# First batch's projection, residual and statistics, and the turned expansion weights, placed in the attention's last steps

## What is computed

```python
x = x + _L0_attn_ref(_layernorm(x), W_attn, W_proj, lambdas)   # differential attention, 16 heads
x = x + _L0_ffn_ref(_layernorm(x), W_syn, b_syn, W_out, b_out, gamma, beta)
...
# in the attention
out = (1.0 - LAMBDA_INIT) * out.reshape(B, T, E)
return out @ W_proj
# in the feed-forward part
z = x_flat @ ternary_quant(W_syn).T + b_syn        # 256 -> 1024
thresh = topv[:, -1:]                              # 102nd largest of each row
hidden = jnp.where(z >= thresh, jax.nn.relu(z), 0.0)
out = hidden @ ternary_quant(W_out).T + b_out      # 1024 -> 256
return layernorm(x + out, gamma, beta)
```

## Time and profile before

| What | Value |
|---|---|
| median of 3 runs | 1247.23 us (1247.14 to 1247.43) |
| the profiled execution, its own time | 1245.16 us |
| its span, first to last instruction | 1243.3 us |
| mean granted TensorE clock | 0.942 of full speed |
| PE busy | 1090.3 us (88%) |
| DVE busy | 908.9 us (73%) |
| ACT busy | 629.1 us (51%) |
| POOL busy | 217.8 us (18%) |

### The profile page before, as it was taken

How to read it: one execution, slowest core, us unless ns; L and a number is a source line. 1 busy time by engine, 2 the same in 40 slices (tenths; PEclk the granted TensorE clock), 3 DMA queues, 4 the chain that set the end, 5 groups by cost and what they waited for, 6 DMA issues and landing times. The chain is left out here.

```text
span 1243.3 us, 18349 instructions
## 1 busy us (share of the span) xinstructions
PE 1090.3 (88%) x7006; PEld 754.3 (61%) x7006; DVE 908.9 (73%) x1699; ACT 629.1 (51%) x1098; POOL 217.8 (18%) x172
## 2 busy tenths in 40 slices
PE   2969999999999878777868569999997899999998
PEld 2823333333333347656757457888886789889986
DVE  7778999999999424689888576555553788897833
ACT  2526878788787852876631133333333433433324
POOL 6004400000000001000033204000000744654400
PEclk9969999999999989998988769999999899999979
DMA  2871133033120010000000111101100100000010
GB/s 93 201 240 31 23 53 52 3 52 52 24 31 3 1 39 1 1 1 1 1 1 1 34 56 34 30 22 35 35 1 15 45 1 1 2 1 1 2 64 6
DMA packets 24850, 40.02 MB, mean 32 GB/s; under 512 B 3116, under 2 KB 12344, under 8 KB 24760
## 3 DMA queue, kind: packets, MB, share of 16 engines
q1 hardware_dynamic: 24760, 38.82, 13.0%
HBM read 28.06 MB, written 10.49 MB: 31 GB/s over the span
## 5 line engine op out<-in xcount | busy, mean ns | idle before, releaser
L667 DVE TENSOR_REDUCE att_mx<-att_ps_m 128x2 f32<-128x1024 f32 x256 | 311.0, 1225 | 23.8 <-PE att_ps_m L561 20.2
L650 ACT ACTIVATE att_prob<-att_ps_s 128x512 f32<-128x512 f32 x512 | 278.2, 596 | 79.3 <-PE att_ps_s L589 66.6
L605 PE MATMUL att_ps_o<-att_prob,v_rows 128*32 128x256 f32 (+1 forms) x1920 | 159.4, 405 | 0.0
L1767 POOL TENSOR_TENSOR qry_prod<-qry_qr,lin_ksum 128x512 f32<-128x512 f32 x64 | 93.8, 1466 | 306.5 <-ACT qry_qr L1888 306.5
L589 PE MATMUL att_ps_s<-qst,kst 50*128 50x512 f32 x512 | 128.1, 496 | 13.6 <-ACT att_prob L650 12.6
L589 PEld LDWEIGHTS att_ps_s<-qst,kst 50*128 50x128 f32 x512 | 48.2, 183 | 126.9 <-ACT att_prob L650 117.2
L561 PE MATMUL att_ps_m<-kst,qst 48*128 48x512 f32 x512 | 110.0, 424 | 9.0 <-DVE att_mx L667 7.2
L1888 ACT ACTIVATE qry_qr<-qry_ps_q 128x512 f32<-128x512 f32 x64 | 38.3, 598 | 131.0 <-PE qry_ps_q L152 114.6
L1468 DVE SCALAR_TENSOR_TENSOR key_k_lo<-key_ps_k,key_k_hi 128x512 fp32r<-128x512 f32 x64 | 44.2, 690 | 67.8 <-ACT key_k_hi L1548 67.3
L605 PEld LDWEIGHTS att_ps_o<-att_prob,v_rows 128*32 128x32 f32 x1920 | 38.2, 108 | 84.5 <-ACT att_prob L650 71.4
L1068 ACT ACTIVATE mlp_junk<-mlp_z,mlp_nlev 128x1024 bf16<-128x1024 f32 x64 | 72.7, 1139 | 23.0 <-DVE mlp_nlev L904 21.5
(11 more groups left out here) (364 smaller groups left out, 2448.2 us busy)
## 6 DMA issues: line engine op xcount, KB each, us to landing
qst<-qk_parts SPq DMA_DIRECT2D x48, 128.0 KB, 4.3
kst<-qk_parts SPq DMA_DIRECT2D x48, 128.0 KB, 6.8
qk_parts<-att_out SPq DMA_DIRECT2D x16, 256.0 KB, 5.5
qk_parts<-qk_lo SPq DMA_DIRECT2D x16, 256.0 KB, 5.7
residual<-L_attn_x SPq DMA_DIRECT2D x4, 512.0 KB, 6.0
lin_wq_raw<-L_attn_Wk SPq DMA_DIRECT2D x4, 512.0 KB, 3.6
lin_wq_raw<-L_attn_Wv SPq DMA_DIRECT2D x4, 512.0 KB, 3.6
lin_wq_raw<-L_attn_Wq SPq DMA_DIRECT2D x4, 512.0 KB, 5.8
```

The lines of the kernel that those rows point to most:

```text
L605: ins = nc.tensor.matmul(ps_o[32 * h:32 * h + 32, cols], vall[:, NS * b + s, h0 + h, :], prob[:, u % PR, h, cols], start=s == 0, stop=s == ...
L650: nc.scalar.activation(prob[:, u % PR, 2 * j + r, :], ps_s[:, (n + r) % BANKS, :], ACT.Exp).then_inc(exp_ok, 1)
L667: nc.vector.reduce_max(mx[:, v % 2, :, m], ps_m[:, n % 2], AX.X).then_inc(m_rd, 1)
L1767: nc.gpsimd.tensor_tensor(prod[:, u % 2, :], qr[:, u % 2, :], ksum[:, b, cols(n)], ALU.mult).then_inc(pr_ok, 1)
```

## The change

A new class `FeedFront` holds, from the attention on, W_proj (`ff.wp`), the turned chunk (`ff.at`), the turned W_syn (`ff.ws_t`) and the norm's work for chunks 0 and 1 (`ff.norms`). Six side units are added to the attention's table, all for buffers `ps_m`: "syn" 0 and 1 in steps 117 and 118, "turn" 0 in step 119, "proj" 0 in 120, "turn" 1 in 121, "proj" 1 in 122. VectorE evacuates each; behind a "proj" it also makes the statistics. W_proj is loaded at the attention's start. The feed-forward stage then has neither the prologue for chunk 0 nor, in step 0, that for chunk 1; it only makes the two roots. It starts with a clearing of the attention's semaphores on SyncE.

```diff
+        u = NS * (HALVES - 1) - LEAD + 1
+        for k in range(d.KT):
+            side[u + k].append(("syn", k, 0))
+        for c in range(ff.CHUNKS):
+            side[u + d.KT + 2 * c].append(("turn", c, 0))
+            side[u + d.KT + 2 * c + 1].append(("proj", c, 0))
...
+                sp.dma_start(ff.wp[:], io["L0_attn_W_proj"].rearrange("(k p) n -> p k n", p=P)).then_inc(wp_in, 16)
                 load_group(1)
...
+                    elif kind == "syn":
+                        pe.wait_ge(tern_ok, 1)
+                        for a in range(d.N // P):
+                            ins = nc.tensor.matmul(ps_m[:, n % 2].rearrange("p r c -> p (r c)")[:, a * P:(a + 1) * P],
+                                                   tern[:, 0, a * d.E + v * P:a * d.E + (v + 1) * P],
+                                                   keep["ident_b"][:], start=True, stop=True)
+                    elif kind == "turn":
+                        for k in range(d.KT):
+                            for j in range(d.TPC):
+                                ins = nc.tensor.transpose(ps_m[:, n % 2, k, j * P:(j + 1) * P],
+                                                          AO[:, d.TPC * v + j, k * P:(k + 1) * P], ident[:])
+                    elif kind == "proj":
+                        pe.wait_ge(wp_in, 16)
+                        pe.wait_ge(m_rd, place("turn", v))
+                        for j in range(d.TPC):
+                            dst = ps_m[:, n % 2].rearrange("p r c -> p (r c)")[:, j * d.E:(j + 1) * d.E]
+                            for k in range(d.KT):
+                                ins = nc.tensor.matmul(dst, ff.at[:, k, j * P:(j + 1) * P], ff.wp[:, k, :],
+                                                       start=k == 0, stop=k == d.KT - 1)
...
+                    elif kind == "syn":
+                        nc.vector.tensor_copy(ff.ws_t[:, v * d.N:(v + 1) * d.N],
+                                              ps_m[:, n % 2].rearrange("p r c -> p (r c)")).then_inc(m_rd, 1)
+                    elif kind == "turn":
+                        nc.vector.tensor_copy(ff.at[:], ps_m[:, n % 2]).then_inc(m_rd, 1)
+                    elif kind == "proj":
+                        rows = X[:, d.TPC * v:d.TPC * (v + 1), :].rearrange("p j e -> p (j e)")
+                        nc.vector.tensor_tensor(rows, rows, ps_m[:, n % 2].rearrange("p r c -> p (r c)"),
+                                                ALU.add).then_inc(m_rd, 1)
+                        dve.wait_ge(m_rd, n + 1)
+                        norm_var(nc, link, ff.norms[v], [X[:, d.TPC * v + j, :] for j in range(d.TPC)])
...
-                sp.dma_start(wp[:], io["L0_attn_W_proj"].rearrange("(k p) n -> p k n", p=P)).then_inc(w_in[0], 16)
+                sp.sem_clear(keep["used"])
...
-                residual(0)
...
-                    if enter is not None and enter + 1 < d.NC:
+                    if enter is not None and FF <= enter + 1 < d.NC:
                         residual(enter + 1)
...
-                attended(0)
-                norm_root(nc, act, w1, 1)
-                for k in range(d.KT):
-                    act.wait_ge(ws_ps, k + 1)
-                    nc.scalar.activation(ws_t[:, k * d.N:(k + 1) * d.N], ps_z[:, k, :], ACT.Copy).then_inc(ws_ok, 1)
+                for c in range(FF):
+                    norm_root(nc, act, ff.norms[c], 1)
...
-                attended(0)
-                turn_syn()
-                project(0)
-                pe.wait_ge(ws_ok, d.KT)
...
-                    if enter is not None and enter + 1 < d.NC:
+                    if enter is not None and FF <= enter + 1 < d.NC:
                         attended(enter + 1)
```

More of the change, by code:

```diff
@@ L418, in load_stack, with __init__ @@
                 sp.dma_start(as_f32(dst[rows]), half).then_inc(sem, 16)
+class FeedFront:
+    CHUNKS = 2
+    def __init__(self, nc, d, ctx):
+        st = Store(nc, ctx, "ff")
+        self.wp = st.sb("wp", [P, d.KT, d.E])
+        self.at = st.sb("at", [P, d.KT, d.CH])
+        self.ws_t = st.sb("ws_t", [P, d.KT * d.N], F32R)
+        self.norms = [NormWork(st, d.TPC, str(c)) for c in range(self.CHUNKS)]
 def stage_attention(nc, d, io, keep, scratch):
@@ L691, in _ @@
                                                 ALU.mult).then_inc(m_rd, 1)
+        assert max(st.sems) - min(st.sems) + 1 == len(st.sems)
+        keep["used"] = range(min(st.sems), max(st.sems) + 1)
 def stage_mlp(nc, d, io, keep):
```

47 lines of the change are left out of this document (21 added, 26 removed).

## The result

| | before | after |
|---|---|---|
| median | 1247.18 us (1245.51 to 1247.84, 6 runs) | 1239.62 us (1236.72 to 1242.86, 6 runs) |
| profiled execution | 1245.16 us | 1239.32 us |
| its span | 1243.3 us | 1237.4 us |
| mean granted clock | 0.942 | 0.949 |

The changed kernel is faster, by a ratio of 0.994 (95% interval 0.9922 to 0.9958), 7.6 us between the medians (5.2 to 9.7 by the interval). The forecast was 12.7 us less, 1234.5 us, with a range from 1232.5 to 1238.5: right in sign, too large in size, and the time is outside the range. The executions of the changed kernel differ among themselves by 6 us. Those of the kernel before differ by 2.3 here, but that is a small sample: in the later sets, of 12 to 18 executions, they differ by 6.2 to 8.8 us.

The account below looks back on a forecast made before the run. ScalarE's exponentials set the pace in the attention's last steps, with TensorE as full; then two chains of waits follow with no engine full. Gains 13.0 + 7.4 less the tail's 7.7 make 12.7 us: 1247.23 to 1234.5 us, range 1232.5 to 1238.5.

Parts of the forecast that it names:

- The tail: Attention's last steps: six side units put between scores and values would cost 7.7 us, lower end 7.0.
- The rival by which units cost their whole length: Attention's last steps: units cost 9.8 instead of 7.7 us, giving 1236.6, or 1237.5 with a wait; chance 0.12.
- First chain: Feed-forward stage's start to first expansion: 22.18 us falls to about 9.2, gain 13.0, between 12.0 and 13.6.
- the choice of 4.4 us for the unused matmuls: Feed-forward stage's start: six unused matmuls, twelve passes, take 4.4 us ahead of the turning, chosen between 2.6 and 4.97.
- a sign of being wrong: Feed-forward stage's start, profile after: ScalarE's copy of b_syn later than TensorE's turning would show the forecast wrong; no size.
- The rival that b_syn's load ends last: Feed-forward stage's start: each us the load ends later than 457 is lost; 1236.5 at 2 us late; chance 0.06.
- this case: Feed-forward stage's start: ScalarE's table load costs 2.6 us, twice its row's 1.30, giving 1235.4; chance 0.04.
- Second chain: Between the feed-forward pipeline's steps 0 and 1: the first level comes 7.4 us earlier, bounds 6.5 and 7.5.
- The sum: Whole kernel: 13.0 + 7.4 - 7.7 = 12.7 us less, with the shift staying whole behind expansion 4.
- The clock rival: Expansions 0 and 4: TensorE at half clock, 1.0 to 2.5 us late, 1235.5 to 1237.0, 1238.0 for both; chance 0.22.
- The base: Whole kernel: 12.7 us taken off the median, 1247.23; the profiled execution, 1245.16 us, lay 2.1 under it.

Follow-up runs that it names:

- a_again: The changed kernel measured again with nothing edited: 1238.33 us, ratio 0.9919 to the kernel before.
- a_ff1: The changed kernel with CHUNKS = 1, so only chunk 0 goes into the attention: 1239.51 us, ratio 0.9937 to the kernel before.
- a_fill: The changed kernel with unused matmuls around the first two turnings raised from 6/4 to 8/8 and 9/7 to 12/13: 1236.92 us, ratio 0.9905 to the kernel before.
- a_d1: The changed kernel behind an extra first block in which VectorE fills 1024 columns of X: 1239.92 us.
- a_d2: The changed kernel behind an extra first block in which VectorE fills 2048 columns of X: 1240.41 us.
- b_d2: The kernel before behind an extra first block in which VectorE fills 2048 columns of X: 1252.05 us, ratio 1.0042 to the kernel before.

## Why the prediction was right or wrong

**The tail, 7.7 us: right.** Measured 8.0 (396.16 - 388.14) and 7.7 in a_again. Of the units, "syn" pays the 0.24 forecast, "turn" 0.71 for 0.68, the first "proj" 3.34 for 3.3. The lower rate of a turning and the place of the second "proj" between two pairs of scores were read correctly from the earlier trace rows, and the evacuations on VectorE were free, as the earlier trace rows said. The rival by which units cost their whole length falls.

**First chain, 9.2 us: right in its steps, 0.4 to 1.1 us long.** Measured 8.77, and 8.07 to 8.18 in the next executions, so 13.4 to 14.1 us gained for 13.0, at or beyond the upper bound of 13.6. The table load with 1.30 us to the root (460.57 to 461.87) has the price of the earlier trace rows. The rows were normalised at 464.49, 3.9 us behind the start. The mis-sized part is the choice of 4.4 us for the unused matmuls: they took 2.83 at full clock, so TensorE waited for the rows, not the rows for TensorE. But then b_syn was the last to come. Its load landed 3.9 us behind its issue and held ScalarE until 464.59, 0.04 us behind the start of the turning, which the prediction had named as a sign of being wrong. ScalarE took the first turned half only when its copy of b_syn ended, at 465.56, 1.01 us behind the turning's start where the earlier trace rows have 0.64, so this cost 0.4 us; in a_again, where the copy began at 464.27, it cost less. The prediction's own terms had ScalarE free (458.1) later than the first half was turned (457.8), and its sum took 462.0 us near that end. The rival that b_syn's load ends last is thus right in kind, and its size is a fraction of a microsecond. The price that the Trainium skill gives for a switch of tables (ScalarE: Activation LUTs, What ACT_TABLE_LOAD costs), 2.66 us with its drain, isn't what this case shows: the load in the open takes 1.28 us and the root starts 1.30 behind its start.

**Second chain, 7.4 us: right where the clock held.** 7.1 us in a_again, 7.3 by giving chunk 1 back (a_ff1). In the trace after only 5.6, since 1.5 us of it went to expansion 0 at half clock.

**The sum: the step that failed is its last sentence**, "Behind expansion 4 every wait is inside the stage or at the meeting of engines, so the shift stays whole." It didn't. Of 12.7 us, the profiled execution after has 11.0 at expansion 4 and 5.9 at the end. The rest of the feed-forward stage took 2.5 us of it and the key stage 1.7, the routed part 1.0, all without any edit in them, the first two with equal counts of matmuls. In the first two TensorE's granted clock changes level at other points of the same work, and the pairs with a late start show that the kernel before has both lengths too, by up to 3.7 us in the rest of the feed-forward stage and 1.9 in the key stage, and that the changed kernel can have the key stage short. The profiled execution of before was at a good position in both, 202.7 and 251.0: in part, then, the forecast started from a lucky sample. What sets the 1.0 us of the routed part stays open; both kernels have both lengths of it.

**The clock rival was the right mechanism, and too small and too narrow.** It had 0.22, was confined to expansions 0 and 4, and gave 1.0 to 2.5 us each. Expansion 0 lost 1.6 us in the trace after and none in a_again; expansion 4 with what follows it some 3.4 in a_again (206.09 - 202.72), which a_fill's unused matmuls bring back (with the later start, 1.7 us: 206.07 to 204.38). What the prediction missed is that the clock falls at another point of the same work when that work starts at another time (a_again and a_d1 above), so that a stage with idle times in it has several lengths. The range of 6 us came from the terms of the edit; the measured executions of the one changed kernel alone cover 6.1 us.

**The base.** The profiled execution of before lay 2.1 us under its median, and was taken for one sample of a steady kernel. In the four comparisons of medians the change is worth 7.6, 9.8, 11.0 and 11.6 us, a mean of 10.0. These four don't contradict each other: by their intervals the first is 5.2 to 9.7 us, the second 7.5 to 12.6. The local gain, the three terms of the sum, is 12.8 to 13.5 us in a_again, a_d1 and a_d2, where expansion 0 kept its clock, and 11.0 in the trace after. The 3 us or so between it and the mean lie behind expansion 4. In the profiles most of them stand in stages in which the clock falls at other points; for the medians, whose other executions weren't traced, this is argued and not shown.

What stays open: whether the first difference of medians (7.6) is smaller than the others by more than chance, since one execution of each set was traced; and how often an execution of the changed kernel has a low stretch in the attention's tail, as a_ff1 had.

**A better version.** a_fill, with more unused matmuls in two steps, is at 1236.92 us, 11.2 us under the kernel before on the same chip, and its five executions differ by only 2.1 us where six of the changed kernel cover 6.1 and 7.3. Between a_fill and a_again (1.4 us) the intervals overlap, and with the later start it is 1.4 us again when each is counted from its own chip's kernel before. It is the best median here, and it isn't shown to be faster than the changed kernel.

## What to carry to other kernels

Work moved from a chain of waits into a stage with one full engine pays its length less that engine's slack, and such a sum can be read from the rows: here to 0.3 us for the tail and 0.4 to 1.1 us for the first chain. What can't be carried through the sum is the time of stages behind it: where the granted clock changes level inside them, their length depends on where in the run they lie, so give each one the spread that its profiles show, and judge a change by pairs with a small delay put ahead of both, with enough executions: three of the kernel before looked steady within 0.3 us, eighteen covered 6.2. Unused matmuls can keep the clock where they end just ahead of the work that sets the pace (a_fill, expansion 4), and cost nearly double where they are queued ahead of it at the lower clock (4.97 us for twelve passes in the earlier trace rows, 2.83 in the trace after).

## What the runs showed of the hardware

TensorE's clock fell to 1.2 GHz in the middle of a stream that was busy for 89% of the 17.6 us before, with a rest of 0.97 us ahead of the first slow row (a_ff1, 10.2 us at 0.50). The same end of the key stage, with the same idle times of 1.15, 2.17 and 0.78 us, came out with a granted clock of 0.63 in its last 12 us (a_again) and of 0.89 (a_d1), and the stage was 2.5 us longer in the first. And a delay of 1.5 us at the very start of the kernel before made its median 4.3 us longer (b_d2, 3.4 to 7.0 by the interval).
